# Numbers of the meeting tiles in one piece behind the first expert tile's product

## What is computed

```python
logits = xf @ Wg.T
probs = jax.nn.softmax(logits, axis=-1)
topw, topi = jax.lax.top_k(probs, K)                      # K = 2 of E = 16
topw = topw / topw.sum(axis=-1, keepdims=True)
gates = (jax.nn.one_hot(topi, E, dtype=xf.dtype) * topw[..., None]).sum(axis=1)
out = jnp.zeros_like(xf)
for e in range(E):
    h = jax.nn.silu(xf @ W1[e]) * (xf @ W3[e])
    out = out + gates[:, e:e + 1] * (h @ W2[e])           # x = x + out
```

## Time and profile before

| | us |
|---|---|
| median of 3 runs | 809.23 |
| the three runs | 807.84 to 809.84 |
| the profiled execution | 807.51 |
| its span | 805.7 |
| TensorE busy | 787.9 (98%) |
| VectorE busy | 590.7 (73%) |
| ScalarE busy | 435.4 (54%) |
| GpSimd busy | 393.1 (49%) |
| mean granted clock of TensorE | 0.995 of full speed |

### The profile page before, as it was taken

One profiled execution on the slowest core, in us unless ns is written; L12 is line 12 of the kernel. 1 busy time (PEld: TensorE's weight loads), 2 busy tenths in 40 slices (PEclk: granted clock), 3 DMA queues, 4 the chain that ended last, 5 costly groups with the idle time before them and its releaser, 6 DMA issues. The chain is left out here.

```text
span 805.7 us, 20983 instructions
## 1 busy us (share of the span) xinstructions
PE 787.9 (98%) x5911; PEld 752.7 (93%) x5912; DVE 590.7 (73%) x1720; ACT 435.4 (54%) x1193; POOL 393.1 (49%) x560
## 2 busy tenths in 40 slices
PE   9999999999999999999999999999999999999995
PEld 8899999999999999999999999999897899999994
DVE  4757778878787878878887878778767566666663
ACT  4473554637273554547373654547255376767773
POOL 2432134543545354544545344544436368687886
PEclk9999999999999999999999999999999999999998
DMA  9786673755647392846657392849779458677780
GB/s 271 253 282 225 224 267 93 278 173 197 242 167 273 109 315 83 285 157 211 228 174 267 122 309 85 289 151 331 271 284 363 134 104 135 120 126 129 132 140 2
DMA packets 105961, 161.19 MB, mean 200 GB/s; under 512 B 10704, under 2 KB 69648, under 8 KB 105040
## 3 DMA queue, kind: packets, MB, share of 16 engines
q1 hardware_dynamic: 80544, 132.89, 48.0%
q0 software_dynamic: 14800, 17.61, 12.1%
q10 hardware_dynamic: 10576, 10.19, 4.7%
HBM read 50.14 MB, written 112.47 MB: 202 GB/s over the span
## 5 line engine op out<-in xcount | busy, mean ns | idle before, releaser
L799 POOL DMA_INDIRECT out<-narrow,sidx x79 | 122.9, 1555 | 46.0 <-DVE sidx L2053 18.7
L1284 ACT ACTIVATE xn3T<-ps 128x512 f32<-128x512 f32 (+1 forms) x18 | 10.3, 574 | 138.9 <-PE ps L819 134.5
L808 PE MATMUL ps<-w_hi,fT_hi 128*128 128x256 f32 x256 | 78.5, 307 | 0.0
L1349 ACT ACTIVATE phi<-ps,nmax 128x128 f32<-128x128 f32 x256 | 73.7, 381 | 8.6 <-DVE nmax L1755 8.6
L1611 DVE TENSOR_TENSOR fT_lo<-relu_v,fT_hi 128x512 fp32r<-128x512 f32 x64 | 54.0, 844 | 32.1 <-ACT relu_v L1363 32.0
L808 PE MATMUL ps<-w_hi,fT_lo 128*128 128x256 f32 x256 | 72.3, 282 | 0.0
L808 PE MATMUL ps<-w_lo,fT_hi 128*128 128x256 f32 x256 | 72.2, 282 | 0.0
L1363 ACT ACTIVATE relu_v<-ps,b_sb 128x256 f32<-128x256 f32 x128 | 69.1, 540 | 0.0
L1362 ACT ACTIVATE fT_hi<-ps,b_sb 128x256 fp32r<-128x256 f32 x128 | 68.1, 532 | 1.0 <-PE ps L808 1.0
L808 PE MATMUL ps<-hT_hi,w_hi 128*128 128x256 f32 x256 | 67.1, 284 | 0.0
L808 PE MATMUL ps<-hT_hi,w_lo 128*128 128x256 f32 x256 | 66.9, 283 | 0.0
(11 more groups left out here) (330 smaller groups left out, 2702.5 us busy)
## 6 DMA issues: line engine op xcount, KB each, us to landing
expert_rows<-zero_rows SPq DMA_DIRECT2D x16, 4352.0 KB, 16.0
narrow<-expert_rows ACTq DMA_DIRECT2D x71, 136.0 KB, 2.5
expert_up_hi<-X SPq DMA_DIRECT2D x16, 352.0 KB, 2.8
e_hi<-expert_up_hi SPq DMA_DIRECT2D x2, 2816.0 KB, 9.9
part_raw<-in_E SPq DMA_DIRECT2D x30, 176.0 KB
expert_up_lo<-part_raw SPq DMA_DIRECT2D x15, 352.0 KB, 3.1
e_lo<-expert_up_lo SPq DMA_DIRECT2D x2, 2464.0 KB, 13.0
X<-in_x SPq DMA_DIRECT2D x16, 256.0 KB, 3.2
```

The costliest lines, as they stand in the source:

```text
L799: pool.indirect_dma_start(out_rows, bass.IndirectOffsetOnAxis(sidx[:, u:u + 1], 0), yg[:, u, :], None, bounds_check=NT * P - 1, oob_is_err ...
L808: return pe.matmul(out_, lhsT, rhs, start=start, stop=stop)
L1284: return act.activation(out_, in_, ACT.Copy)
L1349: last = act.activation(phi[:, g, h, :], ps[:, g, h * M:(h + 1) * M], ACT.Exp, bias=nmax[:, g, h:h + 1])
```

## The change

On TensorE the wait for the gathered edge rows and the two edge products go from the start of slot 1 to behind `up(0, 0)`, ahead of slot 0. They write bank 7 instead of the upper half of bank 1. The wait for VectorE's copy of them goes from slot 3 to slot 1. On VectorE the three steps, in the same order and with the same instructions, go from the ends of slots 1, 2 and 3 to behind `product(0, 0)`, ahead of slot 0.

```diff
             turn_rows(0, 0)
             turn_rows(1, 1)
             up(0, 0)
+            pe.wait_ge(edges_loaded, 16 * 2)
+            for o in range(2):
+                last_mm = mm(ps[0:1, 7, o * P:(1 + o) * P], edge[:, o, D:D + 1], ident[:, :])
+            last_mm.then_inc(edge_ps, 1)
 
             def slot_tiles(s, u, last):
                 if isinstance(s, int) and s == 1:
-                    pe.wait_ge(edges_loaded, 16 * 2)
-                    for o in range(2):
-                        last_mm = mm(ps[0:1, 1, (2 + o) * P:(3 + o) * P], edge[:, o, D:D + 1], ident[:, :])
-                    last_mm.then_inc(edge_ps, 1)
-                if isinstance(s, int) and s == 3:
                     pe.wait_ge(edges_read, 1)
...
             def edge_rows():
                 dve.wait_ge(edge_ps, 1)
-                dve.tensor_copy(edge_row[:, :, :], ps[0:1, 1, 2 * P:4 * P].rearrange("p (o t) -> p o t", o=2)[:, :, 0:SLOT_TILES])\
+                dve.tensor_copy(edge_row[:, :, :], ps[0:1, 7, 0:2 * P].rearrange("p (o t) -> p o t", o=2)[:, :, 0:SLOT_TILES])\
                     .then_inc(edges_read, 1)
                 dve.wait_ge(edges_read, 1)
...
             rows_in(0, 0)
             rows_in(1, 1)
             product(0, 0)
+            edge_rows()
+            meeting_tiles()
+            numbers_of_tiles()
 
             def slot_tiles(s, u, last):
...
                 hidden_in(s, u)
                 scatter_index(s, u)
-                if isinstance(s, int) and s in (1, 2, 3):
-                    (edge_rows, meeting_tiles, numbers_of_tiles)[s - 1]()
```

## The result

Over 20 executions of each, the changed kernel's median is 810.29 us and that of the kernel before 808.11 us (all 20, the three runs shown first among them). The ratio is put at 1.002, 95% interval 1.001 to 1.0029: 1.6 us slower, between 0.8 and 2.3 (the two medians by themselves are 2.2 us apart). That is within the 0.3% that the prediction set as no change, and inside its range; but the sign is clear of noise, and the loss is several times the 0.3 us forecast.

A forecast was written before the change was run, and what follows sets the result against it. TensorE was taken to bound the kernel. A new wait of 0.37 us, VectorE's stall hidden under it, less up to 0.10 given back, was taken as 0.3: 809.23 to 809.5 us, no measurable change; range 807.7 to 811.2.

The forecast's parts named there:

- What bounds the kernel: Expert stage: TensorE, busy 98% of the span, sets the time; its lost microseconds count fully, only the last scatter-adds follow.
- The wait of 0.37 us: Before the edge products: TensorE asks at 634.08, the second gather lands at 634.45, so it waits 0.37 us, up to 0.47.
- the bound from below: TensorE's wait for the gathers could be 0, as landing could be shorter and other executions need not match the profiled one.
- the sum's upper end of 0.5: Whole kernel: the largest slowdown the forecast's sum allowed, 0.5 us, around 0.3 us taken.
- the prediction's own signs: Trace: TensorE idle 0.2 to 0.5 us before the edge matmuls, tile 5's output within 0.5 us; over a microsecond idle refutes.
- VectorE's 1.6 us under the wait: Between tile 0's gate product and tile 2's row split: 1.60 us of number work, hidden, row split 0.2 us early.
- the cleared tiles: Tiles 1 to 4, freed of VectorE's small pieces of number work, give back up to 0.10 us.
- The four matmuls moved for nothing: Edge products on TensorE: four matmuls, 0.52 us of its stream, only moved, neither added nor removed; bank 7 costs nothing.
- The early scatters buy nothing: GpSimd: tile 1's scatter up to 3.75 us earlier, 0.9 if tiles 0 and 1 share a row; no gain at the end.
- S: Theory from the experiments, not the prediction: the early scatter-adds cost time and cause the loss.
- The late-landing rival: Before the edge products: gathers as slow as row stores, TensorE waits 3.3 us more (812.8) or 6.8 (816.3); chance 0.06.
- The backlog rival: Tiles 6 to 74: GpSimd's backlog cost TensorE 3.75 us; removing it all would give 805.8 us; chance 0.04.

The follow-up runs named there:

- late release: Changed kernel, with SyncE also waiting for tile 4's gate product before reading tile 1's numbers, so scatter-adds go out late: 808.94 us, ratio 1.0016 to the kernel before.
- the repeat: The kernel before, run again unchanged: 808.34 against 808.65 us, ratio 0.9993.
- third gather: Changed kernel with an extra, unread gather of 128 rows ahead of the two, TensorE waiting for all three: 812.04 us, ratio 1.0042 to the kernel before.
- filled: Changed kernel with two filler matmul calls between the first up product and the wait for the gathers: 808.92 us, ratio 1.0013 to the kernel before.
- doubled step: Changed kernel with VectorE's comparison step done twice, 0.82 us more: 810.40 us, ratio 1.0017 to the kernel before.
- narrow-gather trace: Changed kernel with each gather cut from whole rows of 1,088 bytes to the one 4-byte number used: 808.95 us, ratio 1.0005 to the kernel before.
- piece in slot 0: Kernel before with VectorE's number work in one piece at the end of slot 0, edge products still at slot 1's start: 808.52 us, ratio 1.0006.

## Why the prediction was right, and where it fell short

**What bounds the kernel**: right. Each microsecond that TensorE lost between tile 0's first product and its output was in the output's time, and at the end the last scatter starts 802.68 - 801.25 - 0.47 = 0.96 us behind its tile's output, as the 0.95 of the earlier trace rows.

**The wait of 0.37 us**: right in its mechanism, too small for the kernel. With row stores that land as early the changed kernel pays 0.42 us (5.54 - 5.12), and that this is so near 0.37 is partly luck. The text read the whole gap from TensorE's question to the landing as a loss, but about 0.2 us of idle stand there without any wait, so 0.37 would have cost some 0.2; and it took the gathers' landing at 3.3 to 3.4 us, while the second took 3.6 in that trace. In its two other traces and in that of the late release the row stores landed 0.8 to 0.9 us later, and it pays 0.90, 0.91 and 1.35, the last with a gather of 3.7 us. The step that failed is the sentence on the bound from below, "the other executions need not be the profiled one": it let the wait be shorter and not longer, and the sum's upper end of 0.5 took only the 3.4 of the gathers' own landing time. What I had not read is that the gathers are issued behind another landing, that of the last row store, whose time has a spread of its own. Why it lands early or late is not known. Tile 0's rows wait for the same landing, but their late arrival was partly hidden by the filler matmuls ahead of tile 0: from the last store's issue to the first up product are 633.17 - 626.55 = 6.62 us with the early landing and 635.16 - 628.30 = 6.86 in the repeat with the late one. TensorE's question moves by 0.24, the answer by 0.88. In the two latest landings, 4.50 and 4.55 us (third gather, filled), the first up product stands 7.14 and 7.75 us behind the store: the question has moved by 0.52 and 1.13 us, the answer by 1.21 and 1.26. So the question can follow, and a still later landing need not make the wait longer.

By the prediction's own signs this was a miss of size: it wanted 0.2 to 0.5 us of idle before the edge matmuls, and said that over a microsecond would make it wrong. The weight loads idle 0.65, 1.13 and 1.13 us in the three traces (the matmuls themselves 0.36, 0.84 and 0.84). Tile 5's output, counted from the first up product, is 0.37, 0.85 and 0.85 us later, against the 0.5 us that it allowed.

The mean of these four traces is (0.42 + 0.90 + 0.91 + 1.35) / 4 = 0.90 us, a ratio of 1.0011. It is a rough figure: three of the four drew the late landing, which only six of all fourteen traces did. The three measurements of the changed kernel, 1.002, 1.001 and 1.0006, all have 1.0011 in their intervals. The first has its middle at 1.6 us, above what any of the traces paid. A longer wait, with a loss of clock behind it, in some of those executions would give that, and so would chance; no such execution was profiled, and which it is stays open. The two slowest of its 20 executions, 812.81 and 813.24 us, do have a mean granted clock of 0.993 against 0.995 for all, but 811.66 us stands at 0.996, and the kernel before has an execution at 811.49 us and 0.992.

**VectorE's 1.6 us under the wait**: right. It is 1.48 us long, no wait of TensorE names it, and the doubled step puts the cover at 0.15 us where the text had "0.2 us early". The copy does wait for the edge products, 0.15 us with the early landing and 0.64 with the late one, where the text had no wait worth a name; as its wait moves with TensorE's, this costs nothing more. Of the up to 0.10 us that the cleared tiles were to give back, 0.05 came: between the outputs of tiles 0 and 5 are 10.06 us before (648.35 - 638.29) and 10.01 after (651.52 - 641.51).

**The four matmuls moved for nothing**: right. With the wait gone, in the narrow-gather trace, the stretch is 5.16 us against 5.12, and from the edge products to tile 0's output are 3.96 us in the first two traces of the changed kernel, whatever their wait.

**The early scatters buy nothing**: right. Tile 1's now starts 644.99 - 643.51 - 0.47 = 1.01 us behind its output, so tiles 0 and 1 do not meet, and S fell with the late release, which is no faster.

**The rivals.** The late-landing rival had the mechanism. It was priced at 3.3 us and more from the gathers' own landing, which stayed between 3.2 and 3.7; the smaller, frequent form through the row stores was not among the cases. In the third-gather run the price was 3.9 us for a wait of 2.3, because of the clock; the forecast had no such term. The backlog rival fell with the piece in slot 0, which has the early scatters and no wait and is not faster (1.0006), and with the 161.1 to 161.2 us from tile 0's output to the last scatter, as before. The rule of the Trainium skill in "DMA: Bandwidth & Descriptors", 2.0 us plus bytes over 436 GB/s, gives estimates of 2.3 and 2.0 us for the wide and the narrow gathers. The traces show 3.2 to 3.7 and 2.7, so by that rule there would have been no wait, and the measurement decides against it.

## What to carry to other kernels

Before a wait is moved ahead of work that covered it, follow the awaited transfer back to what its issue waits for: a spread there is a spread of the wait, and one trace shows only one case of it. Ask too how much of a gap was idle before the wait was there: that part costs nothing new (here 0.2 us). Ask how far the question and how far the answer move when their common cause is late (here 0.24 and 0.88 us). And where the late end of a chain is not what sets the time, as with these numbers, making it earlier gains nothing, and here it cost.

## What the hardware showed that was not expected

- Behind 2.56 us of idle weight loads TensorE's granted clock was 0.66 over the next 5 us, which cost about 1.6 us on top of the wait. Behind 1.58 us of idle it stayed at 1.00, and so it did with five filler matmul calls in a wait that would have been about 1.9 us by our estimate.
- The landing of the last row store is in two groups: in eight of the fourteen traces the first gather is issued 3.28 to 3.30 us behind the store, in six 4.06 to 4.55. (The runs with a third gather count with their first.)
- A gather of 128 rows of 1,088 bytes lands in 3.2 to 3.7 us, one of 128 single numbers of 4 bytes in 2.7.
